# Slots sent pick by pick, and the first loads of slots waiting for fewer picks, in a transformer block with routed experts

## The reference, cut to what matters

```python
group_scores = sg.max(axis=-1); _, gidx = top_k(group_scores, 2)
_, idx = top_k(masked, 4)                      # four experts of each token
w = scores[idx] / scores[idx].sum()
g = silu(x @ W1[e]) * (x @ W3[e]) * w          # for each of the four, inner width 176
y = sum over the four of g @ W2[e]
z = silu(x @ Ws1.T) * (x @ Ws3.T) @ Ws2.T      # the shared expert, inner width 352
x = x + gb * (y + z)
```

## Time and profile before

| what | value |
|---|---|
| median of 3 runs | 1003.52 us (1001.63 to 1004.96) |
| the profiled execution | 1001.45 us, its span 999.6 us |
| sends of slots | 671.3 to 772.4 us |
| shared expert's last tile, routed experts' first | 763.95 and 776.13 us |
| last outer product of an expert | 958.7 us |
| TensorE busy | 869.2 us (87%), mean granted clock 0.938 |

### The profile page before, as it was taken

How to read it: one execution, slowest core, us unless ns; L and a number is a source line. 1 busy time by engine, 2 the same in 40 slices (tenths; PEclk the granted TensorE clock), 3 DMA queues, 4 the chain that set the end, 5 groups by cost and what they waited for, 6 DMA issues and landing times.

```text
span 999.6 us, 19865 instructions
## 1 busy us (share of the span) xinstructions
PE 869.2 (87%) x6994; PEld 738.8 (74%) x6994; DVE 732.2 (73%) x1586; ACT 573.6 (57%) x1072; POOL 657.4 (66%) x625
## 2 busy tenths in 40 slices
PE   5788999999999999999999997649973999999940
PEld 5656777778788888788888786439862899999940
DVE  5777999887978788786879784676842566666648
ACT  1345777778787878887788886523310344444420
POOL 3555878878797888887887985515676355555530
PEclk9999999999999999999999999859985899999975
DMA  8661613233522345232334254333222333333337
GB/s 296 230 133 30 177 31 82 61 64 78 157 50 74 65 98 161 47 83 49 75 67 149 49 159 157 102 76 104 95 107 100 114 118 116 120 116 124 112 122 299
DMA packets 65756, 111.20 MB, mean 111 GB/s; under 512 B 16917, under 2 KB 43292, under 8 KB 63820
## 3 DMA queue, kind: packets, MB, share of 16 engines
q1 hardware_dynamic: 46905, 69.24, 26.0%
q10 hardware_dynamic: 11843, 22.84, 6.5%
q0 software_dynamic: 6912, 17.84, 4.6%
HBM read 46.06 MB, written 39.58 MB: 86 GB/s over the span
## 4 chain that ended last, share of the span: by engine, by line
PE 58%; DVE 11%; POOL 11%; DMA 10%; issue 5%; ACT 3%; SPq 0%; POOLq 0%; ACTq 0%; DVEq 0%
PE bank L680 12%; PE bank L682 11%; PE bank L681 10%; DMA slots<-h,slot_i 7%; PE bank L860 7%; PE bank L1076 7%; POOL p_lo L1912 5%; PE bank L837 4%; POOL turns L1890 2%; PE bank L1048 2%; POOL slots L1969 2%; PE bank L934 2%; DVE nmax L1250 1%; DVE turns L1224 1%; DVE turns L1223 1%
## 5 line engine op out<-in xcount | busy, mean ns | idle before, releaser
L1912 POOL TENSOR_TENSOR p_lo<-p_f,p_hi 128x512 f16<-128x512 f32 x256 | 329.6, 1299 | 46.7 <-ACT p_f L1647 45.8
L1644 ACT ACTIVATE p_hi<-bank,log_up 128x512 f16<-128x512 f32 x256 | 176.1, 688 | 108.2 <-PE bank L682 99.0
L1250 DVE TENSOR_REDUCE nmax<-bank 128x1 fp32r<-128x512 f32 x256 | 174.4, 686 | 86.1 <-PE bank L837 83.0
L1647 ACT ACTIVATE p_f<-bank,log_up 128x512 f32<-128x512 f32 x256 | 175.1, 684 | 15.2 <-POOL p_lo L1912 15.2
L860 PEld LDWEIGHTS bank<-vals,p_hi 128*128 128x128 f16 x2048 | 110.4, 98 | 59.6 <-POOL p_lo L1912 28.6
L860 PE MATMUL bank<-vals,p_hi 128*128 128x66 f16 x2048 | 138.7, 194 | 15.3 <-POOL p_lo L1912 15.1
L1230 DVE TENSOR_TENSOR qk<-rows_f,qk 128x512 fp32r<-128x512 f32 (+1 forms) x128 | 132.6, 1036 | 2.2
L1890 POOL TENSOR_TENSOR turns<-turns 128x512 f32<-128x512 f32 x64 | 90.4, 1414 | 66.0 <-DVE turns L1224 66.0
L680 PE MATMUL bank<-qk 128*128 128x512 f32 x256 | 122.2, 477 | 6.2 <-issue 4.9
L860 PE MATMUL bank<-vals,p_lo 128*128 128x66 f16 x1024 | 121.1, 193 | 0.0
L837 PE MATMUL bank<-qk 128*128 128x512 f32 x256 | 104.2, 410 | 3.8 <-DVE nmax L1250 3.4
(11 more groups left out here) (228 smaller groups left out, 2099.3 us busy)
## 6 DMA issues: line engine op xcount, KB each, us to landing
rows_f<-turns SPq DMA_DIRECT2D x64, 256.0 KB, 3.9
slots<-pad ACTq DMA_DIRECT2D x4, 2880.0 KB, 10.1
h<-slots SPq DMA_DIRECT2D x80, 144.0 KB
w_hi<-parts SPq DMA_DIRECT2D x16, 512.0 KB, 8.3
rows_f<-kl_f SPq DMA_DIRECT2D x32, 192.0 KB, 3.0
w_raw<-in_w ACTq DMA_DIRECT2D x4, 1408.0 KB, 11.8
h_dram<-h_hl SPq DMA_DIRECT2D x3, 1024.0 KB, 4.8
qk<-lat_st SPq DMA_DIRECT2D x16, 192.0 KB, 4.3
```

Source lines behind the costliest of these rows:

```text
L1250: dve.tensor_reduce(nmax[:, k % MAXES:k % MAXES + 1], max_bank[q % 2][:], AX_X, ALU.max, negate=True)\
L1644: act.activation(p_hi[:, u % TB, :], score_bank[u % 2][:], ACT.Exp, bias=log_up[:, 0:1], scale=SCALE)
L1647: act.activation(p_f[:, u % 2, :], score_bank[u % 2][:], ACT.Exp, bias=log_up[:, 0:1], scale=SCALE)\
L1912: pool.tensor_tensor(p_lo[:, u % TB, :], p_f[:, u % 2, :], p_hi[:, u % TB, :], ALU.subtract).then_inc(s_pl, 1)
```

## The change

The sends run pick by pick: pick 0 of all 16 tiles, then pick 1, and so on. The wait for the second half of `slot_i` moves from the seventeenth send to the fifth. `xs` gets a buffer of its own, `ys` moves to `spare` (the memory of `own_f`), and SyncE's wait on `z_x` goes. VectorE forms, for the first sixteen tiles, how far `sent` must have come: 128 times one more than the owner's number, with the number held to 3 at most; SyncE reads it into a register ahead of each of the first sixteen loads and waits for both semaphores. The seventeenth load waits for all sends.

```diff
+EARLY_TILES = 16
+PICK_SENT = 16 * NT // IN_FLIGHT
-        xs = h2_flat[:, 0:CYCLE * XW].rearrange("p (j n) -> p j n", j=CYCLE)
-        ys = h2_flat[:, CYCLE * XW:CYCLE * (XW + D)].rearrange("p (j n) -> p j n", j=CYCLE)
+        xs = sb("xs", [P, CYCLE, XW])
+        ys = spare.rearrange("p (j n) -> p j n", j=CYCLE)
+        sent_for = modT2[:].rearrange("p w c b -> p (w c b)").bitcast(I32)
...
-            sp.wait_ge(listed, 1)
-            for z in range(IN_FLIGHT):
-                sp.wait_ge(sent[z], landed(NT * TOPK, z))
-            sp.wait_ge(z_x, NT)
+            sp.wait_ge(listed, 2)
+
+            def wait_for_slots(m):
+
+                if m < EARLY_TILES:
+                    count = sp.value_load(sent_for[0:1, m:m + 1], min_val=PICK_SENT, max_val=TOPK * PICK_SENT)
+                    for z in range(IN_FLIGHT):
+                        sp.wait_ge(sent[z], count)
+                elif m == EARLY_TILES:
+                    for z in range(IN_FLIGHT):
+                        sp.wait_ge(sent[z], landed(NT * TOPK, z))
...
                 m, jm = n + 3, (j + 3) % CYCLE
+                wait_for_slots(m)
                 if not (static(n) and m < CYCLE):
...
                 dve.tensor_copy(own_i[:, 0:digits], src).then_inc(listed, 1)
+                early = own_f[:, 0:EARLY_TILES]
+                chain(dve.tensor_scalar(early, early, float(TOPK - 1), float(PICK_SENT), ALU.min, ALU.mult))
+                chain(dve.tensor_scalar(early, early, float(PICK_SENT), None, ALU.add))
+                dve.tensor_copy(sent_for, early).then_inc(listed, 1)
...
-            for t in range(NT):
-                if t == TB:
+            for k in range(NT * TOPK):
+                r, t = k // NT, k % NT
+                if k == TB:
                     pool.wait_ge(indexed, 2)
-                for r in range(TOPK):
-                    z, landed = r % IN_FLIGHT, (t * TOPK + r) // IN_FLIGHT
-                    if landed > 0:
-                        pool.wait_ge(sent[z], 16 * landed)
-                    pool.indirect_dma_start(slots, bass.IndirectOffsetOnAxis(ap=slot_i[:, t, r:r + 1], axis=0),
-                                            h2[:, t, :], None).then_inc(sent[z], 16)
+                if k >= IN_FLIGHT:
+                    pool.wait_ge(sent[k % IN_FLIGHT], 16 * (k // IN_FLIGHT))
+                pool.indirect_dma_start(slots, bass.IndirectOffsetOnAxis(ap=slot_i[:, t, r:r + 1], axis=0),
+                                        h2[:, t, :], None).then_inc(sent[k % IN_FLIGHT], 16)
```

## The result

The changed kernel took 996.31 us in the median of 7 runs (990.77 to 1005.66), the kernel before 1001.87 us beside it. The ratio is 0.9923 [0.9897, 0.9949], a gain of 7.7 us of 1003.5, with 5.1 and 10.3 as the ends of its interval. Run again beside the experiments the same kernel came to 0.9896 [0.9871, 0.9922], 10.4 us. One of the seven runs, 1005.66 us, fell into a slower state of the chip and isn't in the ratio. 993.4 us, or 10.1 us of gain, had been forecast; both intervals hold this gain. The median of 996.31 us lies just outside the forecast's own narrow range of 991 to 996, that of the repetition (993.53) inside it. The profiled execution took 992.58 us with a span of 990.8, 8.8 us less than before.

What follows compares the result with a forecast made beforehand. It took the hole before the routed experts, where TensorE waits for all sends, then TensorE's 2.27 us a tile, as the bound. Start 10.1 us earlier, other terms hidden: 1003.5 - 10.1 = 993.4 us, own range 991 to 996, with rivals 984 to 1000.

Steps and rivals of the forecast that it cites:

- (2): Start of routed experts: shared tail and last w_lo (763.95) bind next; first transposes at 766.0, not 776.13, 10.1 us earlier.
- (3): GpSimd's queue: first put stands behind all 64 sends, but ScalarE first waits for one at tile 4; cover 9.2 us.
- (4): New order of sends: pace stays 1.59 us each, last start near 771; bounds 1.26 and 1.99 us.
- (1): First loads of slots: tiles 0 to 3 wait for at most 48 sends, landed by 750.
- (5): VectorE's three added instructions behind own_i: some 0.7 us, hidden by TensorE's slowness there.
- (6): SyncE's added register loads, checks and waits: 0.5 us a tile, first four loads landed by 747.5, 18 us early; costs nothing.
- The tail slow only in this execution: Rival: shared expert's tail runs at its former pace, TensorE ready 12.8 us earlier, 3.6 given back: 984.2 us; chance 0.13.
- The clock back early: Rival: TensorE's clock is full at 766, first tiles take 2.9 us less: 990.5 us; chance 0.14.
- Sends slower: Rival: sends in new order take up to 1.99 us each, GpSimd becomes the bound: 1009.4 us; chance 0.06.
- It doesn't do what it says: Rival: expert 3 owns a first tile or another wait holds SyncE's loads; 1003.5 us less a few tenths; chance 0.08.

Runs made afterwards that it cites:

- the late puts: A memset and six additions on GpSimd between last send and first put: in the kernel after 0.9943 of the kernel before, in the kernel before 0.9998.
- the eight places: Kernel after, with places of their own in ys and sel_i for tiles 0 to 3, waiting for puts only from tile 8: 0.9849 of the kernel before.

## Why the prediction was right, and where it wasn't

The time was right, and the cause of the gain was too: the loads of the first tiles wait for fewer sends. But what stopped the gain at 8 to 10 us is not what step (2) said. By the forecast's own signs (2), (3) and (4) were wrong: the last w_lo isn't near 764, VectorE waits for "parts" in the first ten tiles, and the sends' last start isn't near 771. That the number still fits is partly luck, since two errors met: in the profiled execution the experts started 5.8 us earlier than forecast (760.23 against 766.0), and 7.8 us that the forecast didn't have were lost behind it (5.4 in the wait for put 0, 2.4 at half clock).

**(1) The early wait**: right. The first load is issued at 746.08 and in the repetition at 738.63, where near 742 had been forecast. The run in which the first load waits for all sends lost 8.1 of the 10.4 us.

**(2) The start of the experts**: too late in the forecast. I took the end of the shared tail, 763.95, as given. In the kernel after it was 758.03, in the repetition 747.22, and the experts started at 760.23 and 749.32, not at 766.0. The rival that the tail was slow only in that execution described most of the others: of the eight further profiled executions without the long stall of four in flight, five had the last w_lo at 745.3 to 747.1, and one, of the kernel before with the late puts, at 763.29. That this didn't cost the forecast is the work of the next step.

**(3) GpSimd's order**: the bound was seen, the first to wait was not. I named ScalarE at `ys`, and put its turn for tile 4 against put 0's landing, with 9.2 us of cover. But VectorE waits for the same put before it writes `sel_i` of tile 4, at 789.27 where ScalarE's result of tile 4 is at 794.11: 4.8 us earlier in the pipeline, and with the gT copies of earlier tiles behind it in its queue. The cover was 9.2 - 4.8 = 4.4 us. With the start at 766.0 that would still have been enough (789.27 - 10.1 = 779.2, put 0 due at 774.8). With the true start it wasn't. The landing itself was sized a little too short: put 0 took 2.45 us, not the 2.07 of the earlier trace rows. Together: 4.4 us of cover, less 6.4 since `sel_i` of tile 4 was due at 772.8 and not at 779.2, less 3.4 since put 0 landed at 778.15 and not at 774.8, is -5.4: the wait that was found.

**(4) The pace of the sends**: 1.59 us forecast, (774.4 - 670.4) / 63 = 1.65 found, the last start at 774.4 and in the repetition at 775.7 instead of 771. Where the first load waits for all sends, the same order ends at 769.0. The forecast had no term for this difference, and its cause stays open: of the 6.7 us between that run and the repetition 3.8 are there by the thirty-third send (723.58 against 727.41), before any slot is loaded, so the first tiles can be the cause of the rest at most. If time ahead of put 0 is paid in full, 3 to 4 us here are 3 to 4 us of the kernel.

**(5) VectorE's three instructions**: 0.17 us each, 744.18 - 743.73 = 0.45 us behind `own_i` in place of 0.7; x_hl starts at once behind them. Right, and hidden.

**(6) SyncE**: right. A count's load takes 0.271 us in the median, and no engine waited for slots after the first tile. The pace behind was 2.27 us a tile, as forecast (results of tiles 5 and 6 at 787.67 and 789.93). The last outer product of the kernel before starts at 961.4, not at 958.7 as its table has it; no term hangs on that.

**The rivals.** *The tail slow only in this execution* held for most executions, but its price was computed with the wrong cover: 984.2 came from giving back 3.6 us at ScalarE. With VectorE as the one that waits it gives back 8.4, with the sends 4.3 us later 12.7, and with 2.4 at half clock 15.1: 10.1 + 12.8 - 15.1 = 7.8 us, an estimate at the lower end of the 10.4 [7.8, 12.9] measured. *The clock back early*: it was, 0.83 from 760 to 770 (half clock only until about 765) in place of 0.50, and brought nothing, because the put binds; instead the new stall set it to half once more. *Sends slower* happened in small: a few per cent in place of the 25% of that rival. That sends bind once the cover is gone was its right part: the late puts cost 4.7 us (1.4 to 8.1) for 3.9. *It doesn't do what it says*: no.

## What to carry to other kernels

When an early start is bought on one engine, look for every instruction on any engine that waits for a buffer of the ring to come free, not only for the one that writes the data: the first of them in program order decides, and here it was the one that writes the row numbers. If what frees the ring stands behind a long block of other work on its queue, the early start is worth only as much as the ring is deep; lengthen the ring (15.2 us in place of 10.4) or shorten the block (22.9 with both). And when more transfers of GpSimd's are put in flight, look at what the other engines do meanwhile: here four in flight cost 36 us without pauses, and with a pause every sixteenth send they brought 5.3 us in the kernel before and 7.7 us with the eight places.

## What the runs showed of the hardware

**With GpSimd's transfer queue never dry, the other engines stalled.** With four sends in flight and no pause all of TensorE, ScalarE and VectorE stand for most of 50 us (7.73, 1.69 and 3.32 us busy) with the DMA engines busy for 0.30 of the time; a pause of 2 us every sixteenth send takes this away. The slow tail of the kernel before may be the same in small: the code packet that in the repetition comes at 733.2 comes at 745.0 there, and the last low part at 763.95 instead of 747.22. The other executions go the same way (in the kernel before with the late puts the packet comes near 755 and the last low part at 763.29). Which of the two is late because of the other, the traces don't tell. The queues of the kernel before from 744 to 746.2 us:

```profile
q0 software_dynamic: 80, 0.29, 34.6%
q8 instruction: 1, 0.02, 3.2%
```

By the Trainium skill (Runtime: NRT & Kernel Launch, section "Instruction fetch mechanics") an engine's sequencer refills its instruction memory by a DMA queue of its own in pages of 16 KiB while it runs, and this is hidden by the pace of issue. The size agrees with the packets on q8 (0.02 MB each). If the stalls are waits for code, it isn't hidden here; the traces don't show that they are. What holds the packets back, and what the engines waited for where they went on with no such packet in the trace, stays open.

**Some sends are long beside VectorE's two-input instructions.** Most take 0.96 us; in the kernel after one takes 2.86. GpSimd's row, and VectorE's over the same time:

```profile
700.32 2.86 POOL L1983 DMA_INDIRECT slots<-h,slot_i  x1 [1.20 <-DMA slots<-h,slot_i]
```

```profile
700.36 0.87 DVE L1471 TENSOR_TENSOR w_lo<-w_raw,w_hi 128x704 fp32r<-128x704 f32 x1
...
701.49 0.85 DVE L1449 TENSOR_TENSOR xa<-tiles_of,tab 128x680 f32<-128x680 f32 x1
702.38 0.83 DVE L1451 TENSOR_TENSOR owner<-xa 128x640 f32<-128x640 f32 x1
```

The send ends at 703.18, when the last of these three is done (703.21). With four in flight and no pause, where VectorE nearly stands still, every send that starts from 700 to 750 us takes 0.96 us but one: it starts at 703.00 and takes 1.62 us, beside the w_lo of 702.91. The Trainium skill (SBUF — State Buffer, section "SBUF: two separate sides") says that a VectorE instruction with two inputs from SBUF and a GpSimd instruction that reads SBUF exclude each other from a shared pair of ports, and that whichever starts first holds it for its whole instruction. The rows agree that one is held up beside the other; but the send starts first here, by 0.04 us, and it is the send that is long, so they don't show the order of the rule; no run here took VectorE's work away with the rest unchanged, so it isn't shown as the cause.
